# Four graph networks in one kernel: the third network's dense aggregation as three single-pass products of rounded parts, and the gather's next index copied by ScalarE

## What is computed

```python
def _gcn(x, W, b, row, col, ew):
    x = x @ W
    deg = jax.ops.segment_sum(ew, col, num_segments=n) + 1.0
    dinv = jax.lax.rsqrt(deg)
    norm = dinv[row] * ew * dinv[col]
    agg = jax.ops.segment_sum(norm[:, None] * x[row], col, num_segments=n)
    return agg + (dinv * dinv)[:, None] * x + b

h = jax.nn.relu(x @ Wd + bd) @ Wu + bu + x
h = jax.nn.relu(_gcn(h, W1, b1, row, col, edge_weight))     # 768 -> 256
h = _gcn(h, W2, b2, row, col, edge_weight)                   # 256 -> 768
x = _layernorm(x + h)
```

## Time and profile before

| | |
|---|---|
| median of 3 runs | 3830.29 us (3828.39 to 3833.73) |
| the profiled execution's own time | 3831.38 us |
| its span in the trace | 3829.5 us |
| mean granted clock of PE | 0.944 |
| PE busy | 3419.3 us, 89% of the span |
| PE weight loads busy | 2819.8 us, 74% |
| DVE busy | 2038.9 us, 53% |
| ACT busy | 1230.5 us, 32% |
| POOL busy | 905.5 us, 24% |

### The profile page before, as it was taken

How to read it: one execution, slowest core, us unless ns; L and a number is a source line. 1 busy time by engine, 2 the same in 40 slices (tenths; PEclk the granted TensorE clock), 3 DMA queues, 4 the chain that set the end, 5 groups by cost and what they waited for, 6 DMA issues and landing times. The chain is left out here.

```text
span 3829.5 us, 57503 instructions
## 1 busy us (share of the span) xinstructions
PE 3419.3 (89%) x19326; PEld 2819.8 (74%) x19326; DVE 2038.9 (53%) x3973; ACT 1230.5 (32%) x2195; POOL 905.5 (24%) x992
## 2 busy tenths in 40 slices
PE   4998898998989696999999898999998899599994
PEld 3885454544545365999999788999997767499994
DVE  4987433424333453111587761124878633799996
ACT  1243212212122111111344431113445400278883
POOL 1103755656300000000355530003545300000000
PEclk9988899998999798999999899999999989799997
DMA  2022001000000012334676653335766510100001
GB/s 75 25 64 64 17 1 42 1 25 17 9 16 0 20 34 103 98 98 136 212 239 215 209 172 120 99 101 199 238 216 211 164 56 21 66 1 0 0 0 41
DMA packets 120966, 328.22 MB, mean 86 GB/s; under 512 B 26144, under 2 KB 67661, under 8 KB 120802
## 3 DMA queue, kind: packets, MB, share of 16 engines
q0 software_dynamic: 55408, 208.93, 17.6%
q1 hardware_dynamic: 65394, 117.16, 8.9%
HBM read 243.20 MB, written 82.83 MB: 85 GB/s over the span
## 5 line engine op out<-in xcount | busy, mean ns | idle before, releaser
L585 PE MATMUL bank<-arena 125*125 (+3 forms) x3600 | 762.3, 368 | 0.0
L1430 PE MATMUL bank<-w_hi,xT_hi 128*125 128x384 f32 x1920 | 652.3, 340 | 17.0 <-ACT arena L1218 9.6
L585 PEld LDWEIGHTS bank<-arena 125*125 125x125 f32 x3600 | 497.6, 190 | 229.1 <-issue 176.8
L1431 PE MATMUL bank<-w_lo,xT_hi 128*125 128x384 f32 x1920 | 650.7, 339 | 0.0
L1432 PE MATMUL bank<-w_hi,xT_lo 128*125 128x384 f32 x1920 | 650.7, 339 | 0.0
L1218 ACT COPY arena<-bank 125x384 f32<-125x384 f32 x320 | 153.5, 480 | 807.9 <-PE bank L1432 717.3
L1430 PEld LDWEIGHTS bank<-w_hi,xT_hi 128*125 128x125 f32 x1920 | 358.3, 187 | 18.8 <-issue 12.2
L718 DVE SCALAR_TENSOR_TENSOR row_lo<-arena,edges,row_hi 128x768 fp32r<-128x768 f32 x300 | 304.3, 1014 | 119.4 <-ACT row_hi L685 78.5
L1431 PEld LDWEIGHTS bank<-w_lo,xT_hi 128*125 128x125 f32 x1920 | 358.1, 186 | 0.1
L1432 PEld LDWEIGHTS bank<-w_hi,xT_lo 128*125 128x125 f32 x1920 | 357.9, 186 | 0.1
L1799 DVE CAST w_hi<-w_raw 128x2304 fp32r<-128x2304 f32 x36 | 48.9, 1359 | 562.9 <-PE bank L1432 513.9
(11 more groups left out here) (308 smaller groups left out, 5033.6 us busy)
## 6 DMA issues: line engine op xcount, KB each, us to landing
y_early<-arena SPq DMA_DIRECT2D x200, 187.5 KB
w_raw<-in_L_gnn_W_dram POOLq DMA_DIRECT2D x32, 1152.0 KB
y_late<-arena SPq DMA_DIRECT2D x120, 187.5 KB
arena<-in_L_gnn_W_dram SPq DMA_DIRECT2D x8, 1536.0 KB, 6.8
wadj_d<-arena SPq DMA_DIRECT2D x10, 625.0 KB
arena<-wadj_d SPq DMA_DIRECT2D x1, 6250.0 KB
mask_d<-arena POOLq DMA_DIRECT2D x10, 610.4 KB, 7.5
arena<-mask_d SPq DMA_DIRECT2D x1, 6103.5 KB
```

The lines of the kernel that those rows point to most:

```text
L585: ins = pe.matmul(bank[b][0:P, 0:w], tsc[:, t], f, start=(t == 0), stop=(t == NT - 1))
L1430: pe.matmul(b, xT_hi[:, k, v], w_hi[:, h, k], start=(k == 0), stop=False)
L1431: pe.matmul(b, xT_hi[:, k, v], w_lo[:, h, k], start=False, stop=False)
```

## The change

1. **Rounded parts of the adjacency and of the rows.** For each target block ACT copies `wadj[:, d]` (1280 columns) to `adj_hi[d]`, rounded to fp32r, and DVE subtracts to get `adj_lo[d]`. ACT copies each block of `xs` and `agg1` (256 columns) to `own_hi`, and DVE subtracts to `own_lo`. ACT makes the first five adjacency blocks right after its last transposed copy, then the ten row parts, then the other five adjacency blocks. DVE makes the first five low parts in its loop over `xs`, the other five behind it.
2. **Three products for one.** PE does high x high, low x high, high x low, all in fp32r and 256 columns wide, in place of each float32 product: 600 matmuls for 200.
3. **Finer waits.** PE no longer waits for all of `xs` and all of `agg1`; it waits, in the first target block of each layer, for the low part of each source block, and in c = 0 for `adj_low` of each target block.
4. **DVE adds the own row in two steps** (`own_hi`, then `own_lo`), in place of one addition of `xs` or `agg1`.
5. **The output `agg2`** moves into the first 256 columns of each block of `wadj`.
6. **The gather's next index** is copied by ACT, before it waits for the slot's parts to be free, and not by DVE. POOL now waits for two semaphores ahead of each gather of the loops: `idx_ready` (the index) and `tile_ready` (DVE has read the rows).

```diff
+        next_index(act, k, ...)   in hidden_act and sum_act, ahead of the wait for slot_used
@@ sum_pool
                     pool.wait_ge(idx_ready, (j + past) * GT + (k + 1))
+                    pool.wait_ge(tile_ready, (j + done) * GT + ((HB - 1) * GT + k + 1))
@@ hidden_dve, sum_dve
-                next_index(dve, k, order_idx[:, bass.ds(at + GT, 1), IDX_AT])
@@ scalar
             act_turn(act, "turn_act", xT, KD)
+            act.wait_ge(wadj_loaded, 16)
+            for d in range(ADJ[0][1]):
+                act.copy(adj_hi[d], wadj[:, d].rearrange("p t c -> p (t c)")).then_inc(adj_high, 1)
+            for n in range(NT):
+                act.wait_ge(mm_taken, NT + n + 1)
+                act.copy(own_hi[0][:, n], xs[:, n]).then_inc(own_high, 1)
+            for d in range(ADJ[0][1], NT):
+                act.copy(adj_hi[d], wadj[:, d].rearrange("p t c -> p (t c)")).then_inc(adj_high, 1)
+            for d in range(NT):
+                act.wait_ge(sum_taken, 2 * NT + d + 1)
+                act.copy(own_hi[1][:, d], agg1[:, d]).then_inc(own_high, 1)
@@ tensor
-            pe.wait_ge(wadj_loaded, 16)
-            pe.wait_ge(mm_taken, 2 * NT)
-            for c, own in enumerate((xs, agg1)):
-                if c:
-                    pe.wait_ge(sum_taken, 3 * NT)
+            for c in range(2):
                 for d in range(NT):
                     q = c * NT + d
                     if q >= 4:
                         pe.wait_ge(sum_taken, 2 * NT + q - 3)
+                    if c == 0:
+                        pe.wait_ge(adj_low, d + 1)
                     for t in range(NT):
-                        ins = pe.matmul(bank[q % 4][0:P, 0:G2], wadj[:, d, t, 0:P], own[:, t], start=(t == 0), stop=(t == NT - 1))
+                        if d == 0:
+                            pe.wait_ge(own_low, c * NT + t + 1)
+                        v = slice(t * CT, t * CT + P)
+                        for i, (w, own) in enumerate(((adj_hi[d], own_hi[c]), (adj_lo[d], own_hi[c]), (adj_hi[d], own_lo[c]))):
+                            ins = pe.matmul(bank[q % 4][0:P, 0:G2], w[:, v], own[:, t], start=(t == 0 and i == 0), stop=(t == NT - 1 and i == 2))
                     ins.then_inc(sum_made, 1)
@@ vector
             for n in range(NT):
                 dve.wait_ge(mm_made, NT + n + 1)
                 dve.tensor_scalar(xs[:, n], ...).then_inc(mm_taken, 1)
+                if n < ADJ[0][1]:
+                    adjacency_low(n)
+                if n:
+                    row_low_part(0, n - 1, xs)
+            row_low_part(0, NT - 1, xs)
+            for d in range(ADJ[0][1], NT):
+                adjacency_low(d)
+            def with_own(v, c, d):
+                dve.wait_ge(sum_made, (2 + c) * NT + d + 1)
+                chain(dve.tensor_tensor(v, bank[(c * NT + d) % 4][0:P, 0:G2], own_hi[c][:, d].bitcast(F32), op=ALU.add))
+                chain(dve.tensor_tensor(v, v, own_lo[c][:, d].bitcast(F32), op=ALU.add))
             for d in range(NT):
-                chain(dve.tensor_tensor(agg1[:, d], bank[d % 4][0:P, 0:G2], xs[:, d], op=ALU.add))
+                with_own(agg1[:, d], 0, d)
                 ...
+                if d:
+                    row_low_part(1, d - 1, agg1)
+            row_low_part(1, NT - 1, agg1)
```

More of the change, by code:

```diff
@@ L188, in build @@
         lo_slot = [row_lo[:, i] for i in range(HR)] + [lo_more[:, i] for i in range(HR)]
+        xs_at = w_at + NT * NT * CT
+        mlp_end = fixed + 260 + 2 * D + N + KD * G2
+        gcn_at = -(-(mlp_end + G2) // 16) * 16
+        xT_at = 2 * node
+        ADJ = [(16, 5), (-(-fixed // 16) * 16, 3), (xT_at + NT * G2, 2)]
+        assert sum(n for _, n in ADJ) == NT and 16 + 5 * NT * CT <= node
+        assert ADJ[1][0] + 3 * NT * CT <= mlp_end
+        assert NT * G2 + 2 * NT * CT <= KD * N
+        adj_lo = [placed(f"adj_lo{d}", w_at + d * NT * CT, NT * CT)[0:P] for d in range(NT)]
+        own_lo = [placed("own_lo0", xs_at, NT, G2)[0:P], placed("own_lo1", gcn_at, NT, G2)[0:P]]
+        own_hi = [placed("own_hi0", xs_at + NT * G2, NT, G2)[0:P], placed("own_hi1", xT_at, NT, G2)[0:P]]
+        adj_hi = [placed(f"adj_hi{g}{i}", o + i * NT * CT, NT * CT)[0:P] for g, (o, n) in enumerate(ADJ) for i in range(n)]
         arena = sb("arena", [128, fixed + REST])
@@ L325, in build @@
         gb1_row = cut(rest + 260 + 2 * D + N + KD * G2, G2, parts=P)
-        gcn_at = rest + 260 + 2 * D + N + KD * G2 + G2
         assert gcn_at <= w_at
@@ L334, in build @@
         assert NT * NT * CT <= 6 * HW
[L335 to L338, removed]
+        xs = cut(xs_at, NT, G2, parts=P)
+        assert xs_at + 2 * NT * G2 <= rest + REST
+        agg2 = wadj.rearrange("p d t c -> p d (t c)")[:, :, 0:G2]
         mask_d = dram("mask_d", [N, N])
@@ L400, in build @@
         pool_done = sem("pool_done")
+        adj_high, adj_low, own_high, own_low = sem("adj_high"), sem("adj_low"), sem("own_high"), sem("own_low")
         mm_made, mm_taken = sem("mm_made"), sem("mm_taken")
@@ L661, in sum_pool @@
             past = runs[NT] + 1 if c else 0
+            done = runs[NT] + HB if c else 0
             def body(j, y):
@@ L677, in place_of, with next_index @@
             return nc.s_assert_within(j * GT + (HB * GT + k), 0, NPASS - 1, skip_runtime_bounds_check_because="the last body ends within the table")
+        def next_index(act, k, idx):
+            act.copy(idx_slot[:, k:k + 1], idx).then_inc(idx_ready, 1)
         def hidden_act(act, p, past):
@@ L682, in hidden_act @@
             act.wait_ge(row_landed[k], (past + b + 1) * 16)
+            if b == HB - 1:
+                next_index(act, k, order_idx[:, p + GT, IDX_AT:IDX_AT + 1])
             if p >= HR:
@@ L692, in body @@
                     act.wait_ge(row_landed[k], (j + past + (HB + 1)) * 16)
+                    settle(act)
+                    next_index(act, k, order_idx[:, bass.ds(place_of(j, k) + GT, 1), IDX_AT])
                     act.wait_ge(slot_used, (j + past) * GT + (HB * GT - ring + k + 1))
@@ L706, in sum_act @@
                 between(d)
-        def next_index(dve, k, idx):
-            dve.tensor_copy(idx_slot[:, k:k + 1], idx).then_inc(idx_ready, 1)
         def make_tile(dve, k, before, free, dst, w, hi, lo):
@@ L724, in hidden_dve @@
             make_tile(dve, k, past * GT + p, free, order[:, p, DST_AT:DST_AT + 1], order[:, p, W_AT:W_AT + 1], hi_slot[k % HR], lo_slot[k % HR])
-            if b == HB - 1:
-                next_index(dve, k, order_idx[:, p + GT, IDX_AT:IDX_AT + 1])
         def add_group(dve, bank_at, d, taken, used):
@@ L1889, in _, with adjacency_low, row_low_part @@
             dve.wait_ge(dinv_loaded, 16)
+            def adjacency_low(d):
+                dve.wait_ge(adj_high, d + 1)
+                dve.tensor_tensor(adj_lo[d], wadj[:, d].rearrange("p t c -> p (t c)"), adj_hi[d].bitcast(F32), op=ALU.subtract).then_inc(adj_low, 1)
+            def row_low_part(c, n, own):
+                dve.wait_ge(own_high, c * NT + n + 1)
+                dve.tensor_tensor(own_lo[c][:, n], own[:, n], own_hi[c][:, n].bitcast(F32), op=ALU.subtract).then_inc(own_low, 1)
             for n in range(NT):
@@ L1892, in _ @@
                 dve.tensor_scalar(xs[:, n], bank[6 + n % 2][0:P, 0:G2], dinv[:, n:n + 1], None, op0=ALU.mult).then_inc(mm_taken, 1)
+                if n < ADJ[0][1]:
[9 more added lines that the diff above has]
+                chain(dve.tensor_tensor(v, v, own_lo[c][:, d].bitcast(F32), op=ALU.add))
             for d in range(NT):
-                dve.wait_ge(sum_made, 2 * NT + d + 1)
-                chain(dve.tensor_tensor(agg1[:, d], bank[d % 4][0:P, 0:G2], xs[:, d], op=ALU.add))
+                with_own(agg1[:, d], 0, d)
                 chain(dve.scalar_tensor_tensor(agg1[:, d], agg1[:, d], dinv[:, d:d + 1], gb1_row, op0=ALU.mult, op1=ALU.add))
                 dve.tensor_scalar(agg1[:, d], agg1[:, d], 0.0, dinv[:, d:d + 1], op0=ALU.max, op1=ALU.mult).then_inc(sum_taken, 1)
-            dve.wait_ge(sum_taken, 3 * NT)
+                if d:
+                    row_low_part(1, d - 1, agg1)
+            row_low_part(1, NT - 1, agg1)
             for d in range(NT):
-                dve.wait_ge(sum_made, 3 * NT + d + 1)
-                chain(dve.tensor_tensor(agg2[:, d], bank[(NT + d) % 4][0:P, 0:G2], agg1[:, d], op=ALU.add))
+                with_own(agg2[:, d], 1, d)
                 dve.tensor_scalar(agg2[:, d], agg2[:, d], dinv[:, d:d + 1], None, op0=ALU.mult).then_inc(sum_taken, 1)
```

## The result

| | before | after |
|---|---|---|
| median | 3833.73 us (3828.39 to 3836.17, 5 runs) | 3804.88 us (3803.53 to 3816.25, 5 runs) |
| ratio | | 0.9934, 95% interval 0.9918 to 0.9951 |
| span of the profiled execution | 3829.5 us | 3801.8 us |

The change makes the kernel about 25 us faster by the ratio (0.66% of 3833.7; the two medians are 28.9 us apart); 16.6 were forecast. The median lies 0.1 us under the low end of the range, 3805, although before itself came out 3.4 us above the median that the forecast started from.

What follows compares the result with a forecast made beforehand. PE was taken to bound the aggregation alone, while the gather loops keep it mostly busy. -15.0 - 0.6 - 1.4 + 0.4 + 0 = -16.6 us from 3831.38 gave 3814.8, as a median 3814 us; range 3805 to 3823.

Steps and rivals of the forecast that it cites:

- Part 1: Aggregation sums on PE: 600 single-pass products at 0.120 us, 72.0 us, replace 87.0 us of float32 products; -15.0 us.
- two ways in which I carried the 384-column row over: Price of a 256-column product from 0.1747 us at 384: constant 0.0147 above the columns gives 0.121, proportion to width 0.1165.
- first rival: Aggregation sums: columns alone set the pace, 0.1086 to 0.113 us a product, total 3807 to 3810 us; chance 0.17.
- second rival: Aggregation sums: single-pass products get no faster below 384 columns, 104.8 us for the sums, total 3846 us; chance 0.04.
- Part 2: Finer PE waits: -0.6 us at the start of the sums and -1.4 us between the two layers.
- Part 3: Added ACT and DVE preparation stays covered by PE's work, with 2.8 us slack at the first bank; only a last addition shows.
- thin slack of 0.5: Between the aggregation layers, the last row parts are ready 0.5 to 0.7 us before PE wants them.
- end of the phase: End of the aggregation: one more DVE addition on the last sum, uncovered, +0.4 us.
- Part 4: Gather loops: moving the index copy to ACT about cancels, 0 us, from -5 to +6.
- rival in which the loops gain: Gather loops: DVE's saving and POOL's sooner start add up where PE waits, -4 to -8, 3806 to 3810 us; chance 0.09.
- earlier release of POOL: Gather loops: where the ring runs dry and POOL waits for DVE, POOL goes 0.15 us sooner.
- DVE's 0.07 us a tile: Gather loops: DVE's index copy holds its next operation back by 0.07 us; at most 12.6 us over 180 tiles.

Runs made afterwards that it cites:

- test with 128 columns: The change, with layer one lacking the high adjacency by low rows product and layer two's products in halves of 128 columns; 3880.36 us in one run.
- early copy: The change with the index copy back on DVE, ahead of the low part, POOL waiting for both; 3809.21 us beside 3826.47 for before, ratio 0.9958.
- spare copy: The change with DVE also copying the same index into a spare tile nobody waits for; 3793.77 us beside 3809.80 for before, ratio 0.9960.
- late copy on ACT: The change with ACT's index copy behind the high part, not ahead of it; ratio to before 0.9941 (second chip), 0.9954 (third, 3794.15 us).
- index part alone: The kernel before with only ACT's index copy and POOL's second wait added; 3863.23 us, ratio 1.0116 to before.

## Why the prediction was right, and where it was off

- **Part 1, 600 products for 200: right, 1.0 us too careful.** -15.0 was forecast from 0.120 us a product; 70.97 / 600 is 0.1183, so -16.0. That lies between the two ways in which I carried the 384-column row over, nearer to the proportional one (0.1165). The gap formula of the Trainium skill ("TensorE: Matmul & The Clock Gate", Back-to-back issue gap), which the page gives for a single matmul without a load, makes 0.109 of 256 columns; the trace's 0.118 is 8% above it. The first rival (0.1086 to 0.113) is below it as well. The test with 128 columns adds that half the width still takes 0.109. The second rival, nothing gained below 384 columns, fell.
- **Part 2, finer waits: right.** The first L1541 product begins as the last L1527 ends (3125.76), and there is no gap between the layers. -0.6 and -1.4 were -0.66 and -1.41. The coarse waits were not put back by themselves, so how much of this is theirs is read from the traces alone.
- **Part 3, what is added: covered, as counted.** DVE had taken the first sum 11.0 us after the sums' start (3136.7), where I had 11.6, and PE wanted that bank at 14.2. ACT's wide copies took 1.2 us each and not 1.46. At the layer boundary the last low part was there at 3163.9 and wanted at about 3164.1, so the thin slack of 0.5 was 0.2. DVE in the change, across the first sum:

```profile
3127.92 7.10 DVE L1921 TENSOR_TENSOR adj_lo<-arena,adj_hi 125x1280 fp32r<-125x1280 f32 x5 [0.74 <-ACT adj_hi L1272]
3134.94 0.42 DVE L1942 TENSOR_TENSOR arena<-bank,own_hi 125x256 f32<-125x256 f32 x1
...
3136.38 0.35 DVE L1948 TENSOR_SCALAR arena<-arena,dinv 125x256 f32<-125x256 f32 x1
```

  and ACT, which had been silent:

```profile
3099.20 6.01 ACT L1267 CAST adj_hi<-arena 125x1280 fp32r<-125x1280 f32 x5
...
3126.63 5.90 ACT L1272 CAST adj_hi<-arena 125x1280 fp32r<-125x1280 f32 x5
```

- **The end of the phase, +0.4: right** (0.44 and its signal).
- **Part 4, the index copy: 0 is near its worth over the chips, but not what this stage did.** The stage moved by -9.6 us on the first chip, outside -5 to +6, and this is the term that put the sum off: stretch by stretch, -0.9 (ahead of the second network) - 9.6 + 0.1 - 17.5 + 0.2 are the 27.7 us between the spans. The rival in which the loops gain gave 3806 to 3810, and of its mechanism the earlier release of POOL fell with the early copy. The 0.15 us that the prediction gave that release are 0.07. DVE's 0.07 us a tile agrees with the early copy on the second chip; taken back by the spare copy it was only on a chip that showed no gain, so it stays open. What the prediction missed is that the loops' time differs by as much as 24 us for one and the same kernel between chips. The forecast had one chip's stalls in it and took them for the kernel's. How close the total of 16.6 comes is therefore partly luck: by the ratios the change wins 25 us on the first chip, 10 on the third and 13 on the fourth.
- **The sign, the place and the size** of the main effect were right: 17.5 us in the third network, within 0.3, in each of the traces that have the new aggregation.

No version beats the change beyond doubt. The late copy on ACT was not slower than the change on the one chip where both ran; it would be my choice, for the order and not for a time that I could show.

## What to carry to other kernels

A float32 product that is replaced by three rounded single-pass products wins nearly a fifth of its time (87.0 to 71.0 us) where PE is the only link of the chain and ACT and DVE are idle beside it, if the moving operand is wide enough. Here 256 columns were (0.118 us a product); cut in halves of 128, the same work is twice as many products at 0.109. Count the slack of each part that others must make first, since a shorter PE stage eats it. When an edit moves the time of a stage that it doesn't touch, compare the stretches of several traces, on several chips, before the edit is given the credit or the blame.

## What I had not expected of the hardware

- **Where a loop lies in the program can cost some 40 us** (37 by the medians, 44 by the ratio, 23 in the trace, which is of the fastest of six executions). With the index part alone DVE stood 2.5 to 2.7 us at the head loop's first operation in four turns, 89 packets came over one instruction queue for 68, and the fourth network took 23 us longer in the trace. 53 idle instructions ahead of it put it right. The other kernels of the table, with 68 to 72 packets, have 592 to 598 us there. That the time goes into fetching the loop anew is read from the packets, and not shown by itself.
- **A dense stream can stay at the lower clock.** With 128 columns a product PE was busy without a gap for 121 us at granted clock 0.50, after a wait of 1.4 us. In the same run, with 256 columns, it was at 1.00 after a wait of the same length. It is a single run.
- **The second network, with its gathers, differs between chips** by 24 us of 1540 (1519.5 and 1543.7 for before; its medians, 3810.57 and 3833.73, differ by 23), where the third network's stretch, with a DMA share of at most 0.01 during its sums, agrees within 0.4. Each chip was used at one time only, so it could be the occasion as well as the chip.
